# A retention stage whose pairs pass through five slots instead of three

## The reference, cut to what matters

```
h = h + _L1_attn_ref(_layernorm(h, axis=-1), L1_attn_W_Q, L1_attn_W_K, L1_attn_W_V)
...
# _L1_attn_ref: q = rope(x @ W_Q), k = rope(x @ W_K), v = x @ W_V
#               out = ((q @ k^T) * D) @ v,   D[n, m] = 0.96875 ** (n - m) for n >= m, else 0
```

## Time and profile before

| | |
|---|---|
| time, median of 3 runs | 4524.99 us (4523.86 to 4526.0) |
| profiled execution | 4523.71 us |
| its span, first to last instruction | 4521.8 us |
| mean granted TensorE clock | 0.905 |
| PE busy over the span | 3874.9 us (86%) |
| DVE, ACT, POOL busy | 63%, 51%, 46% |
| retention, first sum to the last output | 856.3 to 1085.6 us |

### The profile page before, as it was taken

The page is one execution under the profiler, slowest core; times in us unless marked ns, Lnnn a source line. Parts: engine busy times, 40 slices in busy tenths (PEclk is TensorE's granted clock), DMA queues, the critical chain, the costliest instruction groups (busy, mean ns, idle before and its releaser), DMA issues.

```text
span 4521.8 us, 111329 instructions
## 1 busy us (share of the span) xinstructions
PE 3874.9 (86%) x31697; PEld 2646.6 (59%) x31697; DVE 2827.4 (63%) x9288; ACT 2307.5 (51%) x5837; POOL 2091.1 (46%) x2436
## 2 busy tenths in 40 slices
PE   7488847677999889999766777999999999899999
PEld 7355523465666656666665444666666666555555
DVE  2577735555788744444344676888888888455554
ACT  5455524211444434444222335888888888555555
POOL 0144337664566422222576563555555555443333
PEclk9999966697999989999655677999999999999999
DMA  1111123222111233333111220000000000233332
GB/s 52 37 31 31 28 50 98 73 56 47 32 37 37 56 82 74 81 80 74 35 42 42 54 51 23 15 12 11 11 11 14 12 11 9 59 76 75 77 78 59
DMA packets 483330, 207.55 MB, mean 46 GB/s; under 512 B 452850, under 2 KB 473326, under 8 KB 482930
## 3 DMA queue, kind: packets, MB, share of 16 engines
q1 hardware_dynamic: 483058, 204.73, 19.9%
HBM read 158.75 MB, written 45.91 MB: 45 GB/s over the span
## 4 chain that ended last, share of the span: by engine, by line
PE 48%; issue 19%; POOL 15%; DVE 9%; SPq 5%; ACT 2%; DMA 1%; POOLq 1%; DVEq 0%; ACTq 0%
POOL att_P L3554 8%; PE sw_pH L4156 5%; PE moe_pH L2714 4%; PE sw_pY L4143 4%; PE moe_pY L2737 4%; DVE att_M L1175 3%; PE att_pS L980 3%; PE moe_pH L2718 2%; PE moe_pH L2724 2%; PE ret_pR L1832 2%; POOL att_norm_rstd L673 1%; PE att_pS L2207 1%; SPq L2881 1%; PE att_pO L1042 1%; SPq L2869 1%
## 5 line engine op out<-in xcount | busy, mean ns | idle before, releaser
L3554 POOL TENSOR_TENSOR att_P<-att_P,att_rden 125x498 f32<-125x498 f32 x512 | 521.0, 1018 | 511.7 <-DVE att_rden L3849 511.2
L3742 ACT ACTIVATE att_P<-att_Z,att_nb 125x249 f32<-125x249 f32 x1024 | 501.5, 494 | 50.8 <-issue 27.9
L2779 DVE TENSOR_TENSOR moe_hT<-moe_silu,moe_pH 128x498 f32<-128x498 f32 x384 | 258.8, 674 | 306.8 <-ACT moe_silu L2763 306.8
L4204 ACT ACTIVATE sw_hT<-sw_pH,sw_b 128x498 f32<-128x498 f32 x512 | 318.3, 673 | 219.4 <-PE sw_pH L4156 219.4
L3663 PEld LDWEIGHTS att_pP<-att_ident,att_P 124*125 124x125 f32 (+1 forms) x2048 | 263.0, 187 | 234.8 <-issue 234.6
L3663 PE MATMUL att_pP<-att_ident,att_P 124*125 124x124 f32 (+1 forms) x2048 | 350.4, 293 | 49.7 <-issue 28.2
L3861 DVE CUSTOM_DVE_ANT_0 att_Z<-att_pS,att_mask 125x249 f32<-125x249 f32 x1024 | 365.8, 412 | 29.5 <-PE att_pS L3651 27.5
L2763 ACT ACTIVATE moe_silu<-moe_pH 128x498 f32<-128x498 f32 x384 | 225.3, 587 | 262.2 <-PE moe_pH L2718 176.3
L3749 ACT ACTIVATE att_PTr<-att_pP 125x498 f32<-125x498 f32 x512 | 296.7, 579 | 76.6 <-PE att_pP L3663 70.3
L2690 POOL TENSOR_TENSOR moe_xe<-moe_share,moe_x 128x1992 f32<-128x1992 f32 x32 | 130.1, 4065 | 427.9 <-DMA moe_share<-mixing 347.6
L4063 POOL TENSOR_TENSOR sw_acc<-sw_acc,sw_Z 128x249 f32<-128x249 f32 x224 | 154.5, 690 | 363.4 <-DVE sw_Z L4283 362.7
(11 more groups left out here) (463 smaller groups left out, 9815.2 us busy)
## 6 DMA issues: line engine op xcount, KB each, us to landing
moe_share<-mixing SPq DMA_DIRECT2D x64, 498.0 KB, 6.1
sw_share<-mixing SPq DMA_DIRECT2D x64, 498.0 KB, 5.6
ffn_W<-in_ffn_pairs SPq DMA_DIRECT2D x64, 192.0 KB, 2.4
att_F<-h_stream SPq DMA_DIRECT2D x192, 62.5 KB
att_X<-h_stream SPq DMA_DIRECT2D x192, 62.5 KB
h_stream<-att_H SPq DMA_DIRECT2D x64, 62.5 KB
ffn_F<-h_stream SPq DMA_DIRECT2D x64, 62.5 KB
ret_F<-h_stream SPq DMA_DIRECT2D x64, 62.5 KB
```

The costliest lines, as they stand in the source:

```text
L3554: g.tensor_tensor(own, own, bc(rden[:, j % 2, c, :], T), ALU.mult).then_inc(*scaled.one())
L3742: ins = a.activation(P[:, r, c, t, :], Z[:, r, c, t, :], ACT.Exp, scale=-1.0, bias=nb[:, r, c, t:t + 1], accum_out=den[:, r, c, t:t + 1])
L4204: a.activation(hT[:, k % 4, :, :], pH[:, place, :, 0:T], ACT.Relu, bias=b1[:, k:k + 1]).then_inc(*hid_ready.one())
```

## The change

`waves` gets five parts instead of three. Part 0, `pre`, now holds only VectorE's sums, in the last step of slot s. Part 1, `even`, has pair s-1: center (GpSimd, step 0), squares (now ScalarE, step 0, by `norm.square_scalar`, line 649, in place of GpSimd), spread (VectorE, step 2), power (GpSimd, step 3). Part 2, `turn_in`, has pair s-2: scale (GpSimd, step 0), transposes (TensorE, step 2, behind the values of the pair in part 4), copy to `xT` (ScalarE, step 3). Part 3, `proj`, has pair s-3: projections, turning, additions, copy of `V`, in the same steps as before. Part 4, `main`, has pair s-4, in the same steps. No buffer is added, and SP's order with its lead of four pairs stays.

```
-    STEPS, WAVES, ROUNDS = 4, 4, 6
+    STEPS, WAVES, ROUNDS = 4, 6, 6
...  gpsimd
-            def pre(n, u, step):
+            def even(n, u, step):
                 if step == 0:
                     g.wait_ge(*xn_ready.before(n))
                     norm.center(g, n, g4(F[:, u, :, :, :]))
-                    norm.square(g, n)
-                if step == 2:
+                if step == 3:
                     norm.power(g, n)
-                if step == 3:
+
+            def turn_in(n, u, step):
+                if step == 0:
                     g.wait_ge(*xT_done.before(n))
                     norm.scale(g, n, g4(xn[:, :, :, :])).then_inc(*xn_ready.one())
-            waves(g, (pre, proj, nothing), STEPS)
+            waves(g, (nothing, even, turn_in, proj, nothing), STEPS)
...  tensor
-            def proj(n, u, step):
-                if step == 0:
+            def turn_in(n, u, step):
+                if step == 2:
                     pe.wait_ge(*xn_ready.after(n))
                     pe.wait_ge(*xT_ready.before(n))
...                  (transposes into pX)
+            def proj(n, u, step):
                 if step == 1:
-            waves(pe, (nothing, proj, main), STEPS)
+            waves(pe, (nothing, nothing, turn_in, proj, main), STEPS)
...  scalar
-            def proj(n, u, step):
+            def even(n, u, step):
                 if step == 0:
+                    norm.square_scalar(a, n)
+            def turn_in(n, u, step):
+                if step == 3:
                     a.wait_ge(*xT_done.after(n))
                     a.wait_ge(*v_done.before(n))
                     a.activation(xT[:, :], pX[:, 0:T], ACT.Copy).then_inc(*xT_ready.one())
+            def proj(n, u, step):
                 if step == 1:
-            waves(a, (nothing, proj, nothing), STEPS)
+            waves(a, (nothing, even, turn_in, proj, nothing), STEPS)
...  vector
             def pre(n, u, step):
-                if step == 0:
+                if step == 3:
                     v.wait_ge(*loaded.after(n, u))
                     norm.sums(v, n, g4(F[:, u, :, :, :]))
+            def even(n, u, step):
                 if step == 2:
                     norm.spread(v, n, 1e-5)
-            waves(v, (pre, proj, main), STEPS)
+            waves(v, (pre, even, nothing, proj, main), STEPS)
```

## The result

The changed kernel takes 4477.99 us (median of 4 runs, 4471.31 to 4481.12) against 4524.42 us of the kernel before (4 runs): a ratio of 0.9902, 95% interval 0.9889 to 0.9916. The forecast was 4477. The profiled execution took 4477.33 us, its span is 4475.6.

What follows compares the result with a forecast made beforehand. It took a ring of waits, 6.6 us a slot, to bound the stage. After the change 28 x 5.2 + 4.86 = 150.5 us replaces 197.6; with 1 us at the start, 48.1 saved from 4523.71, so 4477 (range 4461 to 4500).

Steps and rivals of the forecast that it cites:

- The old ring: Waits from turning through norm, scale, transposes and copy to projections, across VectorE, GpSimd, ScalarE and TensorE: 6.6 us a slot, cut.
- A load that the diff doesn't touch becomes the limit: SP's load of `F`, issued behind store and `X`, would hold up sums and decay: 5.2 us a slot.
- The ring's size: From output through load of `F`, sums, decay, turns and spread to output: 10.4 us for two slots.
- late-load rival: `F` lands 7.2 us after the output instead of 6.3: kernel at 4490 us, chance 0.18.
- TensorE's slot: TensorE's work per slot, from projections to next scores, scores and transposes: 3.54, 0.90 and 0.42, together 4.86 us.
- the first rival: TensorE is the bound because `F` lands within 5.6 us of the output: 4467 us, chance 0.17.
- GpSimd waiting for little: A sign that the forecast holds: GpSimd's waits in the stage would be small; no size given.
- The clock: TensorE's clock dips in the stage would go, clock 1.00; if they stayed, 0.2 us a slot, 6 us.
- The start: Pair 0's output would come 1 us earlier, with one old slot of 6.6 us either way as bounds.
- Squares and the handover: ScalarE's squares, 0.42 us, would be hidden; SP's time from pair 29's store to the next stage's loads, unchanged.
- The rule on a DMA's fixed time: 2.0 us behind the last byte of `F` would make the load 8.0, the slot 6.1, the kernel 4502 us.
- Transfers as the bound: Rival: stores and loads move 374.5 KB a slot at 50 GB/s, slots of 7.5 us, kernel 4544, chance 0.04.

Runs made afterwards that it cites:

- the run with the norm ahead only: The changed kernel with the norm still spread over its own slots, but transposes, copy to `xT` and projections in one slot again: 4520.43 us, ratio 0.9991.
- run for the floor: The changed kernel with the `F` load of n+5 issued ahead of the wait for the output of n: 4454.7 us, ratio 0.9853.
- the four slots: The kernel before with scale, transposes and copy in their own slot, `F` issued before the wait for the output, squares on ScalarE: 4456.76 us, ratio 0.9852.

## Why the prediction was right, point by point

*The old ring goes.* Right, and for the reason given for the transposes: the projections use an `xT` of the slot before. The text gave the norm's own slot as a second cut, and that was not one (the run with the norm ahead only).

*A load that the diff doesn't touch becomes the limit.* Right. The run with `F` ahead of `X` shows it by moving nothing else. The run with the sums behind the decay shows where the late load costs: in the decay behind it.

*The ring's size.* Sum 10.4 us, measured 10.58. Output to landed `F` 6.26 (6.3 taken), decay to the output's end 937.00 - 933.63 = 3.37 (3.37). The sums to the decay took 0.92 in place of 0.62 here: the 0.3 of "issue" in every second slot stands there, and the rows of VectorE's queue in that gap (DVEq, 933.25 and 933.44) name line 698, the loop of `waves`, which closes after two slots. That term was missing. No run took the loop away. Over the stage a slot took 5.33 for 5.2, 3.6 us in 28 slots. (The late-load rival's slot of 5.67 should read 5.65; that is under 1 us of its time.)

*A wrong reason in the working.* I read `F`'s issue, 0.82 behind the end of `X`, as a wait of that slot which would go. It still comes in every second slot after: `F` is issued 0.34 behind the end of `X` in one (938.34 + 0.82 to 939.50), 0.81 in the other (933.29 to 934.10). In the code the `ahead` of every second pair opens SP's loop of two pairs, so I now read that gap as the loop's end and not as a wait; no run tried it, and what it costs by itself was not measured.

*TensorE's slot.* 4.86 was too large: the floor is 4.62. The three stretches that I added overlap at their edges. In the first rival this is 29 x 0.24, 7 us of its 4467. In the sum 4.86 stands only once, for the last slot, since the load ring was longer.

*GpSimd waiting for little* was one of the signs, and it did not come: in 150 us after, its additions still waited 27.8 us for the turning and its centering 18.4 for the sums. GpSimd is in no row of the new ring, though.

*The clock.* Right in the stage: 0.99. *The start* was mis-sized, 4.0 us for 1. The granted clock is one part of it. Stretches after:

```profile
862.00:867.00 5.00, 4.44 (x13) 3.46 (x12) 2.12 (x6) 1.12 (x3) 2.92 (x5) 0.50 0.28 62
868.00:874.00 6.00, 5.74 (x43) 5.16 (x44) 4.40 (x11) 1.37 (x4) 4.81 (x8) 1.00 0.11 23
```

and before, the second of them:

```profile
868.00:874.00 6.00, 4.95 (x17) 3.76 (x18) 2.11 (x4) 0.38 (x1) 2.62 (x5) 0.50 0.06 14
```

TensorE came to 2.4 GHz before 868 in place of after 874, so pair 1's projections no longer ran at 1.2. They stand ahead of pair 0's values; before, then after:

```profile
871.13 3.66 PE L1832 MATMUL ret_pR<-ret_xT,ret_w 128*128 128x249 f32 x8 [0.78 <-ACT ret_xT L1873]
...
869.10 1.95 PE L1835 MATMUL ret_pR<-ret_xT,ret_w 128*128 128x249 f32 x8
```

From the start of pair 0's scores to its first values it was 867.82 to 875.31 before and 868.26 to 871.32 after, 4.4 us less. The clock is some 2.7 of these (scores 0.90 for 1.62, from the projections to the values 2.22 for 4.18). The other 1.7 come with the change's order: before, pair 1's transposes and copy stood between the scores' end at 869.44 and the projections at 871.13; after, nothing does. The scores themselves came 0.4 later. Why the clock rose earlier no run here tells, and it need not be the change: one and the same kernel, run for the floor and again beside the four slots, had pair 0's output at 871.48 in one trace and at 874.67 in the other. The start's gain beyond the forecast, 3.0 us, and the ring's 3.6 us too much nearly cancel: part of the forecast's closeness is luck.

*Squares and the handover.* Right: nothing in this order, and 10.89 us both times.

*The rule on a DMA's fixed time.* The Trainium skill, "DMA: Bandwidth & Descriptors", section "Anatomy of one DMA", gives a fixed 2.0 us for GpSimd's queue, most of it behind the last byte; taken whole behind the last byte it put the slot at an estimated 6.1. The trace of SP's loads of 256-byte rows doesn't bear that out: `F` landed 6.26 us after the output, and its last byte moved not long before. The busy times of the burst before that landing, after a half microsecond in which nothing moved:

```profile
937.50:938.00 0.50, 0.50 (x3) 0.46 (x4) 0.39 (x1) 0.00 (x0) 0.36 (x2) 1.00 0.00 0
938.00:943.00 5.00, 4.99 (x37) 4.48 (x36) 3.44 (x8) 1.18 (x3) 3.78 (x6) 1.00 0.36 79
```

At 79 GB/s the 374.5 KB of store, `X` and `F` had moved by some 942.8, by my estimate, about 0.5 us ahead of the landing at 943.26. The measurement decides.

*Transfers as the bound.* They were not, as the low chance said: 81 GB/s were reached with `F` out of the way.

## What to carry to other kernels

When steps move to a later slot, look for the streams whose order is written elsewhere: a load that is issued behind an output has its lead cut by every slot that the output moves back. Here a new slot cut the ring only where two of its neighbours then stood apart in an engine's order; count places in the queues, not rows of the table. Moving work off an engine is worth what stands behind it in that engine's queue: the same squares, moved the same way, were worth 0 or 16 us.

## What the hardware showed beside this

Rows of 256 bytes moved at 81 GB/s as a mean over 130 us in this stage, with loads and stores mixed, where I had thought of the burst's 77 as near the most. VectorE lost 0.3 us in every second slot that no wait shows, where its queue's rows name the loop that closes there.
